# SyncE fetches one gather's rows in every second block of a DeepFM kernel

## What is computed

```python
first_cat = cat_t1[fidx, cat_feats]
emb_cat = cat_t2[fidx, cat_feats]
emb_cont = cont_t2[None, :, :] * cont_feats[:, :, None]
E = jnp.concatenate([emb_cat, emb_cont], axis=1)
s = jnp.sum(E, axis=1)
fm_second = 0.5 * jnp.sum(s * s - jnp.sum(E * E, axis=1), axis=1)
deep = E.reshape(E.shape[0], -1)
h = jax.nn.relu(_batchnorm(deep @ W1 + b1, g1, be1))
h = jax.nn.relu(_batchnorm(h @ W2 + b2, g2, be2))
deep_out = (h @ W3 + b3)[:, 0]
out_pos = jax.nn.sigmoid(bias + fm_first + fm_second + deep_out)[:, None]
```

## Time and profile before

| | us |
|---|---|
| median of 3 runs | 634.13 (633.69 to 634.48) |
| the profiled execution | 633.67 |
| its span | 631.9 |
| TensorE busy | 571.8 |
| GpSimd busy | 393.8 |
| ScalarE busy | 213.6 |
| VectorE busy | 148.9 |

### The profile page before, as it was taken

One profiled execution on the slowest core, in us unless ns is written; L12 is line 12 of the kernel. 1 busy time (PEld: TensorE's weight loads), 2 busy tenths in 40 slices (PEclk: granted clock), 3 DMA queues, 4 the chain that ended last, 5 costly groups with the idle time before them and its releaser, 6 DMA issues.

```text
span 631.9 us, 8463 instructions
## 1 busy us (share of the span) xinstructions
PE 571.8 (90%) x2531; PEld 460.2 (73%) x2531; DVE 148.9 (24%) x460; ACT 213.6 (34%) x682; POOL 393.8 (62%) x423
## 2 busy tenths in 40 slices
PE   6999899789977997799879987998799999999998
PEld 1588778568866886688658866776678776888887
DVE  1101120013001211130004100311022204754265
ACT  1323132223222322232223222322223315998565
POOL 5777777777777777777777777777777771000000
PEclk9789979998999899998999899979999999999999
DMA  8952334334332343334423432363233321000000
GB/s 265 372 101 27 28 28 27 27 26 28 26 27 27 27 27 27 26 26 27 27 27 26 28 27 26 27 160 27 27 27 28 27 27 9 1 2 0 1 0 2
DMA packets 18251, 26.79 MB, mean 42 GB/s; under 512 B 7827, under 2 KB 8059, under 8 KB 18236
## 3 DMA queue, kind: packets, MB, share of 16 engines
q0 software_dynamic: 13312, 13.87, 27.9%
q1 hardware_dynamic: 4608, 12.66, 5.7%
q10 hardware_dynamic: 316, 0.07, 0.1%
HBM read 26.56 MB, written 0.02 MB: 42 GB/s over the span
## 4 chain that ended last, share of the span: by engine, by line
PE 38%; DMA 26%; issue 16%; POOL 14%; ACT 2%; DVE 2%; POOLq 1%; ACTq 0%; DVEq 0%; SPq 0%
DMA emb<-in_table,idx_now 26%; PE bank L733 15%; PE bank L808 14%; POOL emb L255 14%; PE bank L776 3%; PE bank L707 2%; PE bank L724 2%; ACT junk L293 1%; DVE bank L494 1%; PE bank L844 1%; DMA h<-in_w 1%; PE bank L766 1%; DVE idx_now L477 1%; PE bank L857 1%; PE bank L767 0%
## 5 line engine op out<-in xcount | busy, mean ns | idle before, releaser
L255 POOL DMA_INDIRECT emb<-in_table,idx_now x416 | 393.1, 945 | 129.7 <-issue 118.4
L733 PE MATMUL bank<-x_sb,w_sb 128*128 128x256 f32 x1664 | 391.4, 391 | 2.4 <-ACT x_sb L286 2.4
L733 PEld LDWEIGHTS bank<-x_sb,w_sb 128*128 128x128 f32 x1664 | 320.8, 197 | 46.1 <-ACT x_sb L286 3.6
L293 ACT ACTIVATE junk<-emb 128x128 bf16<-128x128 f32 x208 | 64.2, 309 | 228.4 <-DMA emb<-in_table,idx_now 216.1
L494 DVE TENSOR_TENSOR bank<-emb,bank 128x260 f32<-128x260 f32 x91 | 39.3, 432 | 323.7 <-DMA emb<-in_table,idx_now 323.7
L724 PE MATMUL bank<-ident,emb 128*128 128x128 f32 x208 | 45.1, 301 | 47.7 <-DMA emb<-in_table,idx_now 47.4
L724 PEld LDWEIGHTS bank<-ident,emb 128*128 128x128 f32 x208 | 24.6, 145 | 76.1 <-DMA emb<-in_table,idx_now 66.7
L286 ACT ACTIVATE x_sb<-bank 128x256 f32<-128x256 f32 x104 | 38.6, 371 | 90.4 <-PE bank L724 90.4
L808 PE MATMUL bank<-hhi,w2hi 128*128 128x512 f32 x128 | 50.8, 397 | 0.0
L808 PE MATMUL bank<-hhi,w2lo 128*128 128x512 f32 x128 | 50.4, 394 | 0.0
L808 PE MATMUL bank<-hlo,w2hi 128*128 128x512 f32 x128 | 39.0, 396 | 0.3 <-DVE hlo L605 0.3
(11 more groups left out here) (80 smaller groups left out, 173.6 us busy)
## 6 DMA issues: line engine op xcount, KB each, us to landing
emb<-in_table,idx_now POOLq DMA_INDIRECT x416, 3.3
w_sb<-in_w SPq DMA_DIRECT2D x13, 512.0 KB, 17.4
h<-in_w SPq DMA_DIRECT2D x6, 512.0 KB, 7.5
w2raw<-in_w SPq DMA_DIRECT2D x8, 256.0 KB, 5.5
h<-in_w SPq DMA_DIRECT2D x1, 256.0 KB, 12.3
idx_all<-in_cat SPq DMA_DIRECT2D x1, 182.0 KB, 2.9
cont_sb<-in_cont_t SPq DMA_DIRECT2D x8, 13.0 KB
diag<-in_cont_diag ACTq DMA_DIRECT2D x1, 45.5 KB, 2.1
```

Of the source, the lines that this page charges most:

```text
L255: nc.gpsimd.indirect_dma_start(out=emb[:, j, at:at + ROW], out_offset=None, in_=table, in_offset=bass.IndirectOffsetOnAxis(ap=idx_now[:, j ...
L293: nc.scalar.activation(junk[:, :], emb[:, j, k * PAIR + 1:k * PAIR + 1 + P], ACT.Square, accum_out=esq[:, ds(b * BT + j, 1), k]).then_inc( ...
L733: return nc.tensor.matmul(acc[c], w1_sb[:, k, c * P:(c + 1) * P], x_sb[:, k, :], start=False, stop=stop, skip_group_check=True)
```

## The change

One of the 52 gathers of a block is the held one: k = 12, tile 1, feature 25. In the odd blocks (1, 3, 5, 7) GpSimd leaves it out. SyncE fetches its 128 rows instead, each with a transfer of its own, into a new buffer `row_sb` of 128x65, and VectorE copies that into the slot. In the even blocks GpSimd gathers it as before, but with a semaphore of its own, `rows_gathered`, and VectorE passes that on in `rows_copied`, on which TensorE, ScalarE and VectorE wait for k = 12.

The row numbers come from a new input `cat_rows` of 4 x 128 numbers, which ScalarE's queue loads into a free piece of `h1`. VectorE clamps and offsets them with four operations behind the old index operations and before it releases the indices of k = 4 to 12. SyncE reads them eight at a time into registers. Fetch i is for block 2 i + 1. Fetch 0 stands behind the loads of W1, the others behind the feature load of the block before, once `row_sb` has been copied. VectorE copies after the third of four statistics groups of block 2 i.

```diff
-            with sp.Fori(1, BLOCKS) as b:
+
+            def fetch_rows(i):
+
+                for r0 in range(0, P, ROWS_READ):
+                    _, rows = nc.values_load_multi_w_load_instructions(
+                        rows_idx[0:1, ds(i, 1), r0:r0 + ROWS_READ].rearrange("p a n -> p (a n)"),
+                        engines=(mybir.EngineType.SP,), min_val=0, max_val=CAT * VOCAB - 1,
+                        skip_runtime_bounds_check_because="the vector engine clamps them")
+                    for j, row in enumerate(rows):
+                        p = r0 + j
+                        sp.dma_start(row_sb[p:p + 1, :], table[ds(row, 1), :]).then_inc(rows_landed, 16)
+
+            def cont_load(b):
                 sp.wait_ge(cont_used, b + EMPTY)
                 sp.dma_start(cont_sb[0:CONT, :], cont_t[:, ds(b * BC, BC)]).then_inc(cont_in, 16)
+
+            sp.wait_ge(rows_step, ROWS_STEPS)
+            fetch_rows(0)
+            cont_load(1)
+            with sp.Fori(1, BLOCKS // 2) as i:
+                cont_load(2 * i)
+                sp.wait_ge(rows_copied, 2 * i + 1)
+                fetch_rows(i)
+                cont_load(2 * i + 1)
...
+                            held = (k, j, half) == (ROWS_K, ROWS_J, ROWS_HALF)
+                            if held and rows_elsewhere:
+                                continue
...
-                            ).then_inc(gathered[k], 16)
+                            ).then_inc(rows_gathered if held else gathered[k], 16)
 
             gather(0, AHEAD_FIRST)
-            with pool.Fori(1, BLOCKS) as b:
-                gather(b, AHEAD)
+            with pool.Fori(0, BLOCKS // 2 - 1) as i:
+                gather(2 * i + 1, AHEAD, True)
+                gather(2 * i + 2, AHEAD)
+            gather(BLOCKS - 1, AHEAD, True)
...
+            act.dma_start(rows_idx, cat_rows).then_inc(rows_in, 16)
...
-                act.wait_ge(gathered[k], 16 * 2 * BT * (b + 1))
+                act.wait_ge(gathered[k], 16 * (2 * BT - (k == ROWS_K)) * (b + 1))
+                if k == ROWS_K:
+                    act.wait_ge(rows_copied, b + 2)
...
+            dve.wait_ge(rows_in, 16)
+            x = rows_idx
...
+            nc.vector.tensor_scalar(w, x, 0, VOCAB, ALU.is_lt, ALU.mult).then_inc(rows_step, 1)
+            dve.wait_ge(rows_step, 1)
+            nc.vector.tensor_tensor(w, w, x, ALU.add).then_inc(rows_step, 1)
+            dve.wait_ge(rows_step, 2)
+            nc.vector.tensor_scalar(w, w, 0, VOCAB - 1, ALU.max, ALU.min).then_inc(rows_step, 1)
+            dve.wait_ge(rows_step, 3)
+            nc.vector.tensor_scalar(x, w, (2 * ROWS_K + ROWS_HALF) * VOCAB, None, ALU.add).then_inc(rows_step, 1)
+            dve.wait_ge(rows_step, ROWS_STEPS)
...
+            def copy_rows(i):
+
+                dve.wait_ge(rows_landed, 16 * P * (i + 1))
+                at = ROWS_K * PAIR + ROWS_HALF * ROW
+                nc.vector.tensor_copy(emb[:, ROWS_J, at:at + ROW], row_sb[:, :]).then_inc(rows_copied, 1)
+
+            def whole_block(b, i, odd):
                 for k in range(LEAD, KT):
+                    if k == ROWS_K and not odd:
+                        dve.wait_ge(rows_gathered, 16 * (i + 1))
+                        dve.sem_inc(rows_copied, 1)
                     add_up(b, k)
```

More of the change, by code:

```diff
@@ L47 @@
 EMPTY = 1
+ROWS_STEPS = 4
 NORM_PARTS = [(0, 1), (1, 2), (2, 4), (4, 6), (6, 8)]
 FM_STEPS = 7
+ROWS_READ = 8
+ROWS_K, ROWS_J, ROWS_HALF = KT - 1, BT - 1, 1
 ADDED_EARLY = 8
@@ L52, with build @@
 CROWS = CONT + 1
-def build(nc, table, cat, cont_t, cont_tab, cont_diag, w1, w2, b1_row, params, out):
+def build(nc, table, cat, cat_rows, cont_t, cont_tab, cont_diag, w1, w2, b1_row, params, out):
     f32, f32r = mybir.dt.float32, mybir.dt.float32r
@@ L110, in build @@
     bn1 = place("bn1", [P, 5, C1], f32)
+    row_sb = place("row_sb", [P, ROW], f32)
     kt_bytes = H1 * 4
@@ L127, in build @@
     out_shift = place("out_shift", [P, 1], f32)
+    rows_idx = h1[0:1, C1 - BLOCKS // 2:, BATCH - BC:BATCH - BC + P].bitcast(i32)
     raw = h1[:, :, :].rearrange("p c (s n) -> p (c s) n", n=H1)
@@ L158, in build @@
         slot_open = sem("slot_open")
+        rows_in, rows_step, rows_landed, rows_copied = (
+            sem("rows_in"), sem("rows_step"), sem("rows_landed"), sem("rows_copied"))
+        rows_gathered = sem("rows_gathered")
         m_done, m_ready = sem("m_done"), sem("m_ready")
@@ L241, in _, with gather @@
                                     base=0, pattern=[[-1, P]], channel_multiplier=1).then_inc(ident_made, 1)
-            def gather(b, ahead):
+            def gather(b, ahead, rows_elsewhere=False):
                 for k in range(KT):
@@ L446, in _ @@
             dve.sem_inc(summed, KT)
+            dve.sem_inc(rows_copied, EMPTY)
             nc.vector.memset(eps[:, :], EPS).then_inc(eps_ready, 1)
@@ L484, in _ @@
             find_rows(BT, TILES, idx_all[:, BT * CAT:TILES * CAT].rearrange("p (t f) -> p t f", f=CAT))
+            dve.wait_ge(rows_in, 16)
+            x = rows_idx
+            w = emb[0:1, 1, SCRATCH_KT * PAIR + (TILES - BT) * CAT:][:, 0:BLOCKS // 2 * P].rearrange(
+                "p (a n) -> p a n", n=P)
+            nc.vector.tensor_scalar(w, x, 0, VOCAB, ALU.is_lt, ALU.mult).then_inc(rows_step, 1)
[6 more added lines that the diff above has]
+            dve.wait_ge(rows_step, ROWS_STEPS)
             dve.sem_inc(idx_ready, KT - SCRATCH_KT)
@@ L488, in add_up @@
                 rows = emb[:, :, k * PAIR:(k + 1) * PAIR]
-                dve.wait_ge(gathered[k], 16 * 2 * BT * (b + 1))
+                dve.wait_ge(gathered[k], 16 * (2 * BT - (k == ROWS_K)) * (b + 1))
+                if k == ROWS_K:
+                    dve.wait_ge(rows_copied, b + 2)
                 if k == 0:
@@ L539, in _ @@
                 start_block(0, k)
-            with dve.Fori(0, BLOCKS - 1) as b:
+            def copy_rows(i):
[3 more added lines that the diff above has]
+            def whole_block(b, i, odd):
                 for k in range(LEAD, KT):
+                    if k == ROWS_K and not odd:
+                        dve.wait_ge(rows_gathered, 16 * (i + 1))
+                        dve.sem_inc(rows_copied, 1)
                     add_up(b, k)
@@ L549, in _ @@
                         start_block(b + 1, NEXT_AT[m])
+                    if m == 2 and not odd:
+                        copy_rows(i)
+            with dve.Fori(0, BLOCKS // 2 - 1) as i:
+                whole_block(2 * i, i, False)
+                whole_block(2 * i + 1, i, True)
+            whole_block(BLOCKS - 2, BLOCKS // 2 - 1, False)
             b = BLOCKS - 1
@@ L720, in transpose @@
                     pe.wait_ge(misc_read, b + (1 + EMPTY))
-                pe.wait_ge(gathered[k], 16 * 2 * BT * (b + 1))
+                pe.wait_ge(gathered[k], 16 * (2 * BT - (k == ROWS_K)) * (b + 1))
+                if k == ROWS_K:
+                    pe.wait_ge(rows_copied, b + 2)
                 pe.wait_ge(x_ready, tp_free(b, k))
@@ L884 @@
     cat = np.ascontiguousarray(x["r_cat_feats"].reshape(P, TILES * CAT))
+    tiles = x["r_cat_feats"].reshape(P, TILES, CAT)
+    cat_rows = np.ascontiguousarray(tiles[:, BT + ROWS_J::2 * BT, 2 * ROWS_K + ROWS_HALF].T.reshape(1, BLOCKS // 2, P))
     cont_t = np.ascontiguousarray(x["r_cont_feats"].reshape(P, TILES, CONT).transpose(2, 1, 0).reshape(CONT, BATCH))
@@ L892 @@
     arrays = {
-        "table": table.reshape(CAT * VOCAB, ROW), "cat": cat, "cont_t": cont_t, "cont_tab": cont_tab,
+        "table": table.reshape(CAT * VOCAB, ROW), "cat": cat, "cat_rows": cat_rows, "cont_t": cont_t, "cont_tab": cont_tab,
         "cont_diag": cont_diag.reshape(P, CONT_KT * CONT), "w1": x["W1"], "w2": x["W2"],
```

## The result

The changed kernel takes 659.33 us (657.68 to 660.5), the kernel before 634.31: ratio 1.0394, 95% interval 1.0381 to 1.0406, slower by 25.0 us. The profiled execution took 657.68 us at a span of 655.9, so the spans differ by 24.0. The forecast was 661, with a range from 636 to 709. Ratios here are of undisturbed executions; two executions of the kernel before beside e9_every_w2, at 950 and 1986 us, are left out of its ratio.

A forecast was written before the change was run, and what follows sets the result against it. GpSimd's gathers, 1.249 us each, were taken to bound the kernel until 523 us. 633.67 - 4.0 (gathers removed) + 31.1 (one GpSimd stall, 27.2 plus catching up) = 661 us, range 636 to 709.

The forecast's parts named there:

- GpSimd is the pace: Until 523 us the kernel goes at GpSimd's gather pace, 1.249 us a gather, with TensorE working alone afterwards.
- The gain, 4.0 us: Gathers left out in blocks 1, 3 and 5 save 3.75 us; the one in block 7 only 0.2 to 0.3.
- VectorE's work at nothing: Four index operations, at most 3.0 us and ending near 9 us, and the row copies are covered: zero cost.
- A fetch, 65.3 us: On SyncE, 128 rows at 0.41 us plus 16 register loads at 0.8 us; bounds 45.4 to 98.2 us.
- The features land at 89.1: Block 1's feature load, behind the first fetch on SyncE, lands at L = 89.1; ScalarE needs it at 48.50.
- From there to the 53rd gather, 8.2 us: ScalarE's squares and copy, TensorE's eight products and transposition at low clock; GpSimd released at 97.3, normal cover about 7.5 us.
- Catching up, 3.9 us: After the stop TensorE at low clock runs 1.9 us late, then about 2 us again; total stall 31.1 us.
- forecast case: First fetch delays block 1's features, GpSimd stops once; stall 5.6 us at the low end, about 79 high; chance 0.80.
- Later fetches hidden: The three later fetches cost nothing at 65 us; ScalarE would wait from 81 us, GpSimd from about 101.
- Transfers: Row transfers' 256 small packets per fetch count nothing; queueing behind the weight loads could add up to 15 us.
- Rival 2: Row transfers serialise on their ring, over 101 us a fetch; all four stop GpSimd, 857 us at 1.0 a row; chance 0.10.
- Rival 3: Fetch up to 40.8 us, so L + 5.5 (GpSimd's release at full clock) stays under 70.1: 629.7 us; chance 0.07.

The follow-up runs named there:

- e9_every_w2: e1_order with fetches for blocks 1 to 7, 32 row numbers per register load, W2 loads moved behind the first fetch: 629.97 us, ratio 0.9911.
- e6b_no_last: e7_order_again without GpSimd's last three gathers, those of k = 12 in block 7: 630.88 us, ratio 0.9942 to the kernel before.
- e1_order: Changed kernel with block 1's feature load ahead of the first row fetch on SyncE: 630.68 us, ratio 0.9948 to the kernel before.
- e7_order_again: The same kernel as e1_order, run again as reference for a later run: 630.28 us, ratio 0.9939 to the kernel before.
- e4_loads32: Changed kernel with four register loads of 32 row numbers per fetch instead of sixteen of 8: 654.68 us, ratio 1.0325.
- e8_split72: Changed kernel with 72 of the first fetch's 128 rows ahead of block 1's feature load, the rest behind: 630.52 us, ratio 0.9939.
- e2_split96: Changed kernel with 96 of the first fetch's rows ahead of block 1's feature load, 32 behind it: 641.44 us, ratio 1.0129.

## Why the prediction was right, step by step

**GpSimd is the pace.** Right. Outside the two stops the gathers stand 1.248 to 1.249 us apart, and the sum for the last gather closes to 0.1 us.

**The gain, 4.0 us.** Right, and for the reason given: 5.0 at the last gather, 4.0 at the second layer, and e6b_no_last shows the end flat. The comparisons of e1_order and e7_order_again, where no stop covers the gain, have it at 3.3 and 3.9.

**VectorE's work at nothing.** Right. The four operations ended at 9.4 us against "near 9"; the copy took 0.18 us where it did not wait.

**A fetch, 65.3 us.** Nearly right. Measured 67.2, from the first register load at 20.6 to the feature load at 87.8. The parts, in the changed kernel:

```profile
L242 SPq FUSED_REGOPS  x512: 37/37/51, 21.4 to 441.2; - x171
L242 SPq MOVE row_sb<-in_table x512: 29/29/38, 21.5 to 441.3; - x171
L242 SPq DMA_DIRECT2D row_sb<-in_table x512: 224/225/311, 21.6 to 441.4; - x171
```

```profile
30.35 3.13 SPq L242 DMA_DIRECT2D row_sb<-in_table  x8
```

The transfer instruction is cheaper than I had it, 0.225 and not 0.31. Neither the thirteen-row load of SyncE nor the one-row load of ScalarE's queue was a good row for it; why both cost more is not shown. In return there is one instruction more, 0.029, and the gaps are wider. From row to row it comes to (3.13 - 0.225) / 7 = 0.415 us, against 0.41: the total was right while the parts were off in both directions. The register load was 0.688 against 0.8. The Trainium skill ("DMA: Bandwidth & Descriptors", section "Latency and other measured facts") gives a floor of about 0.6, and the trace agrees for eight numbers; that it grows by 56 ns a number is from these runs alone.

**The features land at 89.1.** ScalarE took them at 89.32. The fetch was 1.9 us longer but began 0.9 earlier, at 20.6, and the landing was shorter: 1.5 us from the start of the issue to ScalarE's square and not 2.3.

**From there to the 53rd gather, 8.2 us.** Measured 8.2 (89.32 to 97.54), again from parts that cancel. The products took 5.2 us (90.87 to 96.11) and not 6.2. That is luck of this execution in part: in e4_loads32 they took 6.3 and in e8_split72 6.1. The sum had no time between the end of a transposition and the start of the gather that it releases, and this is 97.54 - 96.49 = 1.05 us. For the same reason the cover was not 7.5 us but 70.06 - 62.50 - 0.38 - 1.05 = 6.1.

**Catching up, 3.9 us.** This is the term that was mis-sized: 0.6 was measured. I had taken the long stretch at the low clock at the start of the old trace as the measure of what comes after idling. The windows of the changed kernel (from:to, busy by engine, granted clock, DMA) show that it ended within some 5 us of new work, which began at 90.87:

```profile
90.00:96.00 6.00, 5.13 (x16) 4.29 (x17) 0.00 (x0) 3.31 (x18) 0.00 (x0) 0.64 0.01 3
96.00:120.00 24.00, 24.00 (x116) 20.39 (x114) 4.66 (x16) 7.69 (x29) 16.70 (x18) 0.96 0.30 23
```

So only the eight products behind the stop went partly at 1.2 GHz, and not the next slots. With 0.6 for this term the sum would have been 633.67 - 4.0 + 27.2 + 0.6 = 657.5, against 657.68 profiled.

**The range.** Its lower end of 636 lies 0.7 above what the low end of the forecast case adds up to, 633.67 - 4.0 + 5.6 = 635.3. Nothing hangs on it.

**Later fetches hidden.** Right: at 67 us each they are far from the 81 where ScalarE would wait, and the list of waits has that wait once.

**Transfers.** Right. SyncE's queue has 5632 packets where it had 4608: 1024 more for 512 rows, two each. The first fetch, behind the weights, took 66.21 us and a later one 66.18. The hold of up to 15 us that the upper end allowed for did not occur.

```profile
q1 hardware_dynamic: 5632, 12.79, 5.7%
```

**Rival 2, rows that serialise.** Did not happen. In e1_order the last row was issued by 97.69, and VectorE's copy, which waits for all 128, started at 98.69: the last row had landed about 1 us after its issue, with the others in flight beside it. The fixed 2.0 us that the prediction quotes from the Trainium skill ("DMA: Bandwidth & Descriptors", section "Anatomy of one DMA") are given there for transfers issued by GpSimd, and these come from SyncE; the measured 0.415 us a row and 1 us to landing decide here.

**Rival 3, faster.** Its condition was named rightly, block 1's features in time, and e1_order and e8_split72 meet it by moving the load instead of shortening the fetch: 630.7 and 630.5 against the 629.7 it was given. Its bound was too wide, though. L + 5.5 took the full clock and no time before the gather, and e8_split72 measured L + 9.1, so the features had to land by 61.0 and not by 64.6. At that bound the fetch would have had to be 37 us long and not 40.8, which makes the faster case less likely than the prediction had it.

## What to carry to other kernels

When work is put on an idle queue, ask first what stands behind it in that queue and who takes that, and only then who waits for the new work: here VectorE could wait 14 us for the rows at no cost that the trace shows, and one small load behind them stopped GpSimd for 28 us. SyncE works through its program in order, idle or not; its idle time is slack only for work that is placed behind the loads that others need. And a gain on the pacing engine counts only up to the point where the next engine has no wait left: three gathers less at the end were worth nothing, three more in the middle less than half.

## What the runs showed of the hardware

- A register load on SyncE took 240 ns and 56 ns for each number (688 ns for 8, 2034 for 32), and a transfer of one row at a register's address went every 0.415 us, with 0.225 for the transfer instruction.
- GpSimd's gathers came at one of two paces, one to an execution. In the profiled executions of the kernel before, the changed one and six of the experiments they stood 1.248 to 1.249 us apart (stops left out); in those of e1_order, e6b_no_last and e9_every_w2 it was 1.251, from the first fifty to the last. e1_order and e7_order_again are the same program and had one pace each. Over 412 gathers this is about 1.0 us, as much as some of the effects here. Why is open.
- From the end of the releasing transposition to the start of the gather it took 1.04 to 1.05 us, before the 53rd gather of the changed kernel, e2_split96, e4_loads32 and e8_split72.
- The eight products behind a stop of TensorE, 3.5 us long at the full clock, took 5.2 us after 33 us without work, 5.1 after 15 (e2_split96), 6.3 after 29 (e4_loads32) and 6.1 after only 5 (e8_split72): the price of the low clock did not grow with the length of the stop. At the start of the kernel before, the granted clock stayed at 0.50 from 23 to 36 us. Before that, from 5.9 to 19.7 us, TensorE had done 28 products (`h` with `diag`), with the clock at 1.00. Why the low clock lasted so much longer there is open.
